# Causal mask of the row-maximum pass: an identity matmul on TensorE in place of the fused add-and-max on VectorE

## What is computed

```python
scores = jnp.einsum('bsd,de,bte->bst', input_data, qk, input_data) / SCALE
causal = jnp.tril(jnp.ones((S, S), dtype=bool))
scores = jnp.where(causal, scores, -jnp.inf)
attn = jax.nn.softmax(scores, axis=-1)
return jnp.einsum('bst,btd,de->bse', attn, input_data, ov)
# and, of the whole:
x = x + _L0_attn_ref(xn, ...) + _L0_ffn_ref(xn, ...)     # xn: the rows normalised
```

## Time and profile before

| | |
|---|---|
| median of 3 runs | 234.03 us (233.63 to 234.73) |
| the profiled execution | 234.73 us, of which the span 232.6 us |
| busy of the span | PE 220.1, DVE 177.2, ACT 160.6, POOL 113.2 us |
| units of the row-maximum pass | 80, from 21 to 167 us |
| DVE in the 48 plain units | 31.9 us |
| DVE in the 32 masked units | 15.5 us, and 2.6 us of accumulator reads |

### The profile page before, as it was taken

How to read it: one execution, slowest core, us unless ns; L and a number is a source line. 1 busy time by engine, 2 the same in 40 slices (tenths; PEclk the granted TensorE clock), 3 DMA queues, 4 the chain that set the end, 5 groups by cost and what they waited for, 6 DMA issues and landing times.

```text
span 232.6 us, 7007 instructions
## 1 busy us (share of the span) xinstructions
PE 220.1 (95%) x2510; PEld 171.3 (74%) x2510; DVE 177.2 (76%) x479; ACT 160.6 (69%) x366; POOL 113.2 (49%) x158
## 2 busy tenths in 40 slices
PE   8699999999998999999999999999999999999993
PEld 5464375878777768666548798999999998777672
DVE  5998989699799476989998889766645654458954
ACT  3979999872165997765558645766667667777592
POOL 8648569675047777776300034566547566100000
PEclk9859999999999999999999999999999999999999
DMA  5993521999501111111193001321111111391821
GB/s 168 305 238 92 158 71 30 190 135 120 65 3 57 53 43 48 45 48 45 45 272 88 1 14 37 94 68 47 48 32 54 47 35 48 111 252 27 254 65 45
DMA packets 30960, 20.93 MB, mean 90 GB/s; under 512 B 2088, under 2 KB 28752, under 8 KB 30928
## 3 DMA queue, kind: packets, MB, share of 16 engines
q1 hardware_dynamic: 28320, 15.68, 30.3%
q0 software_dynamic: 2272, 4.67, 6.3%
q10 hardware_dynamic: 336, 0.14, 0.2%
HBM read 11.15 MB, written 9.34 MB: 88 GB/s over the span
## 4 chain that ended last, share of the span: by engine, by line
PE 70%; ACT 9%; DVE 7%; issue 6%; DMA 3%; POOL 3%; SPq 1%; DVEq 0%; ACTq 0%; POOLq 0%
PE psum L1355 5%; PE psum L1357 5%; PE psum L1356 5%; PE psum L1332 5%; PE psum L1399 5%; PE psum L1400 4%; PE psum L1390 4%; PE psum L1407 4%; PE psum L1504 4%; PE psum L1532 4%; PE psum L1531 4%; PE psum L1530 4%; PE psum L1506 4%; PE psum L1505 4%; PE psum L1477 2%
## 5 line engine op out<-in xcount | busy, mean ns | idle before, releaser
L687 POOL DMA_INDIRECT sorted_y<-xn,store x39 | 37.5, 960 | 47.9 <-ACT xn L1222 38.2
L1083 ACT ACTIVATE p_sb<-psum 128x512 f32<-128x512 f32 (+1 forms) x80 | 41.8, 537 | 14.7 <-PE psum L1390 14.6
L677 POOL DMA_INDIRECT sorted_x<-xn,pos x32 | 33.7, 1052 | 22.7 <-DVE pos L847 11.3
L936 DVE TENSOR_TENSOR p_lo<-p_sb,p_hi 128x512 f16<-128x512 f32 (+3 forms) x56 | 33.7, 617 | 14.3 <-ACT p_sb L1083 14.2
L1077 ACT ACTIVATE p_hi<-psum 128x512 f16<-128x512 f32 (+3 forms) x56 | 30.2, 546 | 18.8 <-PE psum L1407 9.0
L1051 DVE SCALAR_TENSOR_TENSOR h_lo<-psum,h_hi 128x512 f16<-128x512 f32 x39 | 26.6, 687 | 13.1 <-ACT h_hi L1215 12.9
L1215 ACT ACTIVATE h_hi<-psum 128x512 f16<-128x512 f32 x39 | 23.3, 597 | 17.5 <-PE psum L1506 16.9
L921 DVE TENSOR_REDUCE row_max<-psum 128x1 f32<-128x512 f32 x48 | 31.9, 683 | 3.7 <-PE psum L1332 3.5
L1355 PE MATMUL psum<-qT_hi,kT_hi 128*128 128x512 f16 (+1 forms) x80 | 27.8, 348 | 1.1 <-ACT p_sb L1083 1.1
L1504 PE MATMUL psum<-x2T,w_hl 128*128 128x128 f16 x156 | 28.0, 219 | 0.3 <-issue 0.3
L1530 PE MATMUL psum<-w_hl,h_hi 128*128 x156 | 28.1, 219 | 0.0
(11 more groups left out here) (210 smaller groups left out, 567.0 us busy)
## 6 DMA issues: line engine op xcount, KB each, us to landing
w_raw<-in_L_ffn_w SPq DMA_DIRECT2D x16, 256.0 KB, 3.5
sorted_x<-zero SPq DMA_DIRECT2D x1, 2515.5 KB, 23.1
xn<-sorted_x SPq DMA_DIRECT2D x8, 258.0 KB, 4.9
x_sb<-in_L_attn_input_data SPq DMA_DIRECT2D x8, 256.0 KB, 5.6
xn<-sorted_y SPq DMA_DIRECT2D x8, 256.0 KB, 4.9
out<-x_sb SPq DMA_DIRECT2D x6, 256.0 KB, 2.6
sorted_y<-xn,store POOLq DMA_INDIRECT x39, 2.2
sorted_x<-xn,pos POOLq DMA_INDIRECT x32, 2.5
```

The costliest lines, as they stand in the source:

```text
L687: pool.indirect_dma_start(out=sorted_y[:, :], out_offset=bass.IndirectOffsetOnAxis(ap=store[:, t:t + 1], axis=0), in_=xs[:, t % SLOTS, 0:P ...
L1083: a.activation(p_sb[:, u, off:GW], bank[SCORE[n % R]][:, off:GW], ACT.Exp, scale=SCALE).then_inc(s_exp, 1)
```

## The change

The mask of the 32 diagonal units moves from DVE to PE. PE adds a second matmul to each such unit: `ident16` as weights, the new constant `mask_qk` (128 x 128, -1e30 above the diagonal) as the moving operand, accumulated onto the unit's last 128 columns; the semaphore is signalled by this second one. DVE uses the plain reduction for all 80 units. The constant `late_keys` (512 columns, two POOL instructions) becomes `mask_qk` (one), and `masked` is gone. The list `ORDER` is as it was.

```diff
-    N_EARLY = 9
+    N_EARLY = 8
...
-        late_keys = sb("late_keys", [P, GW], BF16)
-        masked = sb("masked", [P, GT * (GT + 1) // 2 * P], F16)
+        mask_qk = sb("mask_qk", [P, P], BF16)
...
-            pool.memset(late_keys[:, 0:GW - P], 0.0).then_inc(s_const, 1)
-            pool.affine_select(out=late_keys[:, GW - P:GW], in_=zero[:, 0:P], compare_op=ALU.is_ge, fill=MASK, base=0,
+            pool.affine_select(out=mask_qk[:], in_=zero[:, 0:P], compare_op=ALU.is_ge, fill=MASK, base=0,
                                pattern=[[-1, P]], channel_multiplier=1).then_inc(s_const, 1)
...
-                if c == g:
-                    at = i * (i + 1) // 2 * P
-                    v.wait_ge(s_const, N_EARLY)
-                    if b or g:
-                        before = ("MR",) + ((b, g - 1) if g else (b - 1, BG - 1))
-                        v.wait_ge(s_max, nth[before + (i, before[2])] + 1)
-                    v.tensor_tensor_reduce(out=masked[:, at:at + w], in0=bank[bank_of[unit]][:, 0:w], in1=late_keys[:, GW - w:GW],
-                                           op0=ALU.add, op1=ALU.max, scale=1.0, scalar=MASK,
-                                           accum_out=row_max[:, i, c:c + 1]).then_inc(s_max, 1)
-                else:
-                    v.tensor_reduce(row_max[:, i, c:c + 1], bank[bank_of[unit]][:, 0:w], AX.X, ALU.max).then_inc(s_max, 1)
+                v.tensor_reduce(row_max[:, i, c:c + 1], bank[bank_of[unit]][:, 0:w], AX.X, ALU.max).then_inc(s_max, 1)
...
-                w = (i + 1) * P if c == g else GW
+                diag = c == g
+                w = (i + 1) * P if diag else GW
...
-                mm(at[:, 0:w], qT_hi[:, q:q + P], kT_hi[:, k:k + w], start=True, stop=True).then_inc(s_mm, 1)
+                m = mm(at[:, 0:w], qT_hi[:, q:q + P], kT_hi[:, k:k + w], start=True, stop=not diag)
+                if diag:
+                    m = mm(at[:, w - P:w], ident16[:], mask_qk[:], start=False, stop=True)
+                m.then_inc(s_mm, 1)
```

## The result

| | |
|---|---|
| time after, first comparison | 236.55 us median of 4 (235.79 to 238.23) |
| time before, beside it | 233.88 us median of 4 (233.63 to 234.73) |
| all 15 executions of the first comparison | 235.79 to 239.43 us; without the longest, median 237.5 |
| ratio, by the mean of those 14 | 1.0141 (1.0098 to 1.0185), +3.3 us |
| three later comparisons of the same kernel | 1.0044 (1.0025 to 1.0062), 1.0049 (1.0022 to 1.0076), 1.0044 (1.0025 to 1.0063) |

The account below looks back on a forecast made before the run. PE was taken to bound the kernel (busy 220.1 of 232.6 us). 13 paid masks x 0.056 = 0.73 us, less 0.03 from DVE, gave +0.7 us: from the median 234.03 to 234.7 us, range 233.7 to 235.9.

Parts of the forecast that it names:

- What bounds the kernel: Whole kernel: PE bounds it, busy 220.1 of 232.6 us, clock 1.00; added PE work is paid unless a wait absorbs it.
- DVE's half: 32 diagonal units on DVE: accumulator read overlaps its successor, plain form saves 0.3 us in all, 0.03 on the chain.
- The pitch of the mask: Each added mask matmul on PE takes 56 ns, not the skill's 81 ns.
- Which are paid: Of the 32 mask matmuls on PE, 13 lengthen the kernel, 0.73 us; waits absorb the others.
- the stretch where the chain steps over to DVE: Near 109 us: two units at 108.9 paid, DVE getting both delays; four paid in 102 to 109 us.
- So 32 x 0.056 = 1.79 us on PE: All 32 diagonal units: the added mask matmuls take 1.79 us of PE time, weight loads hidden.
- All 12 are absorbed: 0: 20 to 52 us: the first 12 units' masks, 0.67 us on PE, vanish in PE's waits and cost nothing.
- (a): Rival, all masks: absorbing waits slide along, 21 to 32 units paid, 1.2 to 1.79 us, 235.2 to 235.8; chance 0.2.
- (b): Rival, 52 to 168 us: short waits absorb all, 0 to 0.3 us, 234.0 to 234.3; chance 0.2.
- (c): Rival, where DVE sets the pace: the accumulator read costs its 81 ns, so faster, 233.8 or 232.7 us; chance 0.1.

Follow-up runs that it names:

- e2: Kernel before plus the 32 mask matmuls on PE, DVE keeping its fused add-and-max: 1.0033, 235.08 us.
- e3: Changed kernel without the 32 mask matmuls, so row maxima of the diagonal units are unmasked: 0.9976, 233.57 us.
- after: The changed kernel's profiled execution in the first comparison, no further edit: span 233.3 us; that comparison's median of four was 236.55 us.
- e6: Changed kernel with each mask matmul issued twice: 1.0133, 237.5 us.
- e12: Kernel before with 24 matmuls of 8 columns on zeros, each with its load, added on PE between no. 449 and no. 705: 1.0067, 235.94 us.
- e13: Changed kernel with 24 matmuls of 8 columns on zeros, each with its load, added between no. 449 and no. 705: 1.0190, 239.04 us.
- e9: Changed kernel with its 24 warm-up matmuls of 256 columns joined into 12 of 512, 24 PE instructions fewer: 1.0034.
- e15: Repeat of e9 (changed kernel, 12 warm-up matmuls of 512 columns for 24 of 256): 1.0016, 234.67 us.
- e4: Kernel before with the change made only in the first 12 diagonal units (first three groups of batch 0): 1.0016.
- e7: Changed kernel run again, unaltered, against the kernel before: 1.0049.
- e8: Kernel before with its 24 warm-up matmuls of 256 columns cut into 48 of 128, 48 PE instructions more: 1.0020, 234.87 us.
- e11: Changed kernel with the zero-fill of `sorted_x` issued at 46 us instead of 40.5: 1.0065, 235.62 us.

## Why the prediction was wrong

**What bounds the kernel: right.** PE full in every stage, clock at 1.00, the loss comes with PE's part (e2) and not from DVE's.

**DVE's half: right in the mechanism.** The read overlaps: 0.03 us over four fused units between 103 and 109 us. The effect of e3 was 0.6 us (0.1 to 1.0 by its interval) where I had at most 0.3; with the masks in, none of it is left to see.

**The pitch of the mask: right.** 56 ns, not 81.

**Which are paid: nearly right, with one item wrong.** Forecast 0.73 us, measured 0.53 to 0.65 between 51.8 and 168.8 us. By stretch, in the first trace of after: up to 73.8 us +0.17 (forecast 4 x 0.056 = 0.22; it had been +0.29, and a wait at 73.8 took 0.11 back). From 92 to 101.6 +0.19 (forecast 0.17). From 101.6 to 120 +0.06 (forecast 0.22, less DVE's 0.03): of the four I counted about one is paid. From 120 to 168 +0.15 (forecast 0.11). The mis-sized item is the stretch where the chain steps over to DVE: PE's lag is taken in by a DVE that waits less afterwards, and the chain now leaves DVE at 114 us.

**The step that failed: "So 32 x 0.056 = 1.79 us on PE"**, the cost of an added instruction taken as its time on the engine and nothing else. An added matmul also is two instructions in PE's program and moves every later one towards its block boundary. The kernel before reached the boundary at 705 with some 2 us to spare, behind the largest transfer of the program; "All 12 are absorbed: 0" was therefore no free entry. PE came to the boundary up to 1.9 us sooner (51.4 to 51.8 instead of 53.36), so small delays of that block that were harmless now stop PE. e6 (a standstill of 1.66 us beside 0.54 us more of matmuls paid later) and e12 against e13 (1.7 against 3.6) show the mechanism. Its share in the plain change is 0 to 0.48 us in four traces, and some 0.5 by e9 and e15 if their medians are taken at their word. This fits the +1.1 us of the later comparisons. It does not explain the first one.

**The rivals.** (a) gave 235.2 to 235.8, and two of the three later medians lie in it, the third just below. Its reason isn't seen behind 52 us, where 0.53 to 0.65 us are paid and all 20 masks would be 1.12. Ahead of 52 us it is open: PE's waits on `row_max` ahead of the unit's matmul fell from 2.6 + 1.8 to 3.2 us, as absorbed masks would have it, while e4's median leaves room for some of the 0.67. (b) and (c) are out for the full change: their 234.3 us and less was reached by none of its medians. What I lacked was a rival in which an instruction costs its place in the program.

**What stays open** is the first comparison's further 2 us (+3.3 against +1.1): twelve of its fourteen executions are longer than the longest of the 34 later ones (236.10 us). It is of the size of a late block: 1.66 us in e6's standstill, 2.68 and a dropped clock in e13. But the four traces of the changed kernel have spans of 232.9 to 233.3 us, shorter than any of the first comparison's, and none shows the block arriving that late. That it was the fetch is argued, not shown; that something else differed in that session is a rival that no run excludes. Open too is what delays the block more in one execution than in another: in `after` it ended at 47.74 us, in e7 at 50.14.

Part of the scatter is common to all kernels and sits earlier: ACT's wait for the last expert weights near 43 us was 0 to 1.0 us over the traces.

## What to carry to other kernels

In a long unrolled program an instruction costs its place as well as its time: look at the profile's instruction queue, find where each 256th instruction of the fullest engine falls (its semaphore instructions counted too), and ask whether a large transfer holds the DMA engines at the time when that block is sent for. An engine's idle time by "issue" ahead of an ordinary matmul, above all within one loop of matmuls, is the sign of it. Matmuls that look absorbed by a wait for another engine are only free if no such boundary comes behind them; and taking a fused mask off DVE gains nothing when DVE's form was no slower than the plain one.

## What was not expected of the hardware

- A block of PE's program, whose packet ended 1.6 us after no. 449 in e8 (38.20 to 39.82), ended 7 to 12 us after it where a transfer of 2515.5 KB lay between, and could run 1.4 to 1.7 us after its packet's end.
- PE stands for it 0.31, 0.47, 0.61, 1.66 and 2.68 us in five kernels (e7, e8, e11, e6, e13), in e8 and e13 between two matmuls of one loop.
- After 2.68 us of standstill the granted clock fell to 0.56 for 3.9 us; after 1.66 us it stayed at 1.00.
- Twenty-four idle matmuls of 8 columns, 0.76 us of PE's time, cost 1.7 us in one kernel and 3.6 in a nearly identical one.
